# Second cross attention of a four-layer block: from seven slots a unit to four phases a unit

## The reference, cut to what matters

```python
q = layernorm(x, ln_q_g, ln_q_b) @ Wq * scale
k, v = jnp.split(media @ Wkv, 2, axis=-1)
sim = jnp.einsum('bhid,bhjd->bhij', q, k)
sim = jnp.where(media_mask[:, None, None, :], sim, neg_inf)
attn = jax.nn.softmax(sim, axis=-1)
out = jnp.einsum('bhij,bhjd->bhid', attn, v)
```

## Time and profile before

| what | value |
|---|---|
| time, median of 3 runs | 3631.37 us (3630.75 to 3647.57) |
| span of the profiled execution | 3628.6 us |
| the profiled execution's own time | not listed apart; its span is 2.8 us under the median |
| TensorE busy | 3390.8 us, 93% of the span |
| VectorE, ScalarE, GpSimd busy | 2019.1, 1846.1, 1589.9 us |
| second cross attention | from about 1633 to 3045 us of the span |

### The profile page before, as it was taken

The page is one execution under the profiler, slowest core; times in us unless marked ns, Lnnn a source line. Parts: engine busy times, 40 slices in busy tenths (PEclk is TensorE's granted clock), DMA queues, the critical chain, the costliest instruction groups (busy, mean ns, idle before and its releaser), DMA issues. The chain is left out here.

```text
span 3628.6 us, 74082 instructions
## 1 busy us (share of the span) xinstructions
PE 3390.8 (93%) x25048; PEld 2305.3 (64%) x25048; DVE 2019.1 (56%) x3324; ACT 1846.1 (51%) x3374; POOL 1589.9 (44%) x1421
## 2 busy tenths in 40 slices
PE   7798799898999799989999999999999998999997
PEld 5556544344444388866666666666666666878886
DVE  4465577776777454435555555555555553114454
ACT  2254277676776533335555555555555553333333
POOL 3213012221221011107777777777777775005554
PEclk9899799999999899999999999999999999999998
DMA  4784200000000222220000000000001003220200
GB/s 120 170 131 120 79 7 18 17 17 17 17 18 27 96 74 100 107 112 10 13 31 14 32 13 32 16 30 15 33 29 42 13 13 119 82 75 1 98 7 12
DMA packets 74751, 179.36 MB, mean 49 GB/s; under 512 B 14720, under 2 KB 44928, under 8 KB 68480
## 3 DMA queue, kind: packets, MB, share of 16 engines
q1 hardware_dynamic: 70240, 161.81, 14.7%
q0 software_dynamic: 4128, 12.60, 1.3%
HBM read 115.09 MB, written 59.26 MB: 48 GB/s over the span
## 5 line engine op out<-in xcount | busy, mean ns | idle before, releaser
L1654 POOL TENSOR_TENSOR cross_acc<-cross_acc,cross_probs 128x512 f32<-128x512 f32 (+1 forms) x704 | 921.4, 1309 | 159.9 <-ACT cross_probs L1717 118.6
L1717 ACT ACTIVATE cross_probs<-cross_s,cross_bias 128x512 f32<-128x512 f32 (+1 forms) x832 | 530.3, 685 | 488.9 <-PE cross_s L1936 487.1
L1813 DVE TENSOR_REDUCE cross_partmax<-cross_r 128x1 f32<-128x400 f32 (+1 forms) x1024 | 541.2, 570 | 334.3 <-PE cross_r L1906 316.0
L1256 DVE TENSOR_REDUCE cross_partmax<-cross_m 128x2 f32<-128x800 f32 (+1 forms) x512 | 497.0, 991 | 187.1 <-PE cross_m L1359 186.1
L1167 ACT ACTIVATE cross_probs<-cross_s 128x512 f32<-128x512 f32 (+1 forms) x832 | 453.9, 596 | 150.7 <-PE cross_s L1379 150.4
L1949 PE MATMUL cross_av<-cross_probs,cross_v 128*64 128x256 f32 (+1 forms) x3328 | 459.1, 394 | 0.0
L1949 PEld LDWEIGHTS cross_av<-cross_probs,cross_v 128*64 128x64 f32 (+1 forms) x3328 | 199.5, 136 | 173.2 <-ACT cross_probs L1717 77.3
L1106 POOL TENSOR_TENSOR cross_diag<-c_ident,cross_negmax 128x256 fp32r<-128x256 f32 x128 | 76.0, 615 | 497.6 <-DVE cross_negmax L1264 497.6
L1390 PE MATMUL cross_av<-cross_probs,cross_v 128*32 128x256 f32 (+1 forms) x3328 | 269.0, 395 | 10.2 <-ACT cross_probs L1167 9.0
L1802 DVE TENSOR_TENSOR cross_k_lo<-cross_r,cross_k_hi 128x400 fp32r<-128x400 f32 (+1 forms) x256 | 146.4, 572 | 192.4 <-ACT cross_k_hi L1695 192.4
L1930 PE MATMUL cross_s<-cross_q_hi,cross_k_hi 64*128 64x256 f32 (+1 forms) x1664 | 253.0, 299 | 0.0
(11 more groups left out here) (307 smaller groups left out, 6479.6 us busy)
## 6 DMA issues: line engine op xcount, KB each, us to landing
d_masked_ctx<-tail_ctx_split SPq DMA_DIRECT2D x8, 1602.0 KB, 5.3
d_self_qk<-selfproj_qk_split POOLq DMA_DIRECT2D x32, 256.0 KB, 5.5
self_qs<-d_self_qk SPq DMA_DIRECT2D x64, 128.0 KB, 8.0
self_ks<-d_self_qk SPq DMA_DIRECT2D x64, 128.0 KB, 8.5
d_cross<-tail_pr SPq DMA_DIRECT2D x8, 1024.0 KB, 4.6
cross_qp<-d_cross SPq DMA_DIRECT2D x64, 128.0 KB, 2.4
d_cross<-cross_out SPq DMA_DIRECT2D x64, 128.0 KB, 1.8
tail_attn<-d_cross SPq DMA_DIRECT2D x8, 1024.0 KB, 5.5
```

The source lines that it names most:

```text
L1256: nc.vector.tensor_reduce(partmax[:, :, jt // 2, jt % 2, i:i + 1], m_pair(sets[q], w), AX.X, ALU.max).then_inc(maxed, 1)
L1654: nc.gpsimd.tensor_tensor(acc[0:w, g % 2], left, probs[0:w, slot % NPB], ALU.add).then_inc(added, 1)
L1717: nc.scalar.activation(probs[0:w, (g * KT + t) % NPB], src_, ACT.Exp, scale=XHD ** -0.5, bias=bias[0:w, p, t:t + 1]).then_inc(probs_ready, 1)
L1813: nc.vector.tensor_reduce(partmax[:, m, i:i + 1], r_ps[MAX_BANK[q]][:, 0:KCH[i][1]], AX.X, ALU.max).then_inc(maxed, 1)
```

## The change

The unit is cut in four phases of two score sets each instead of seven slots, on all three engines. The sets are now ranges of two or one tiles, so that the groups 0 to 3, 4 to 6, 7 to 9 and 10 to 12 fill the phases, and a set's buffer is `s_ps[s % 2]`. On TensorE phase k runs: maxima 4k and 4k+1; scores of set 2k; maxima 4k+2 and 4k+3; scores of set 2k+1; value products of the group in front (in phase 0 those of the unit before, followed by its sums); in phase 3 the shift; key chunk k of `after`; one value tile. Keys now always use bank 1, value tiles bank 2, shift and sums bank 0. The start-up code keeps its banks, apart from the first scores, which move to phase 0. GpSimd and SyncE keep their order, and no instruction is added or dropped.

```diff
-        SETS = [range(t, min(t + 2, KT)) for t in range(0, KT, 2)]
+        SETS = [range(lo, hi) for lo, hi in ((0, 2), (2, 4), (4, 6), (6, 7), (7, 9), (9, 10), (10, 12), (12, 13))]
+        GROUPS = [range(0, 4), range(4, 7), range(7, 10), range(10, 13)]
-        K_BANK, V_BANK, SHIFT_BANK, SUM_BANK = (2, 1, 0, 2), (0, 2, 0, 1), 1, 1
-        MAX_BANK = (0, 1, 2, 0, 2, 0, 1, 2, 1, 2, 0, 1, 0, 1, 2, 0)
-        v_at, k_at = {1: (0,), 4: (1,), 6: (2, 3)}, {2: 0, 3: 1, 4: 2, 5: 3}
+        K_BANK, V_BANK, SHIFT_BANK, SUM_BANK = (1, 1, 1, 1), 2, 0, 0
+        MAX_BANK = (0, 1, 2, 0) * 4
```

ScalarE:

```diff
+                def phase(u, nxt, k, before):
                     after = nxt and following(nxt, NP)
+                    for s in (2 * k, 2 * k + 1):
+                        for t in SETS[s]:
+                            exponential(u, s, t)
+                    if after:
+                        k_high(after, k)
+                    made = value_tile(u, k)
+                    if made:
+                        v_tile(*made, r_ps[V_BANK])
+                    if before:
+                        copy_av(before)
+                        inverse_sum(before)
```

VectorE, in `step(u, nxt)`:

```diff
+                    for k in range(NQ):
+                        for q in range(4 * k, 4 * k + 4):
+                            maxima(nxt, q)
+                        if k == NQ - 1:
+                            diagonals(nxt)
+                            copy_shift(nxt)
+                        if after:
+                            k_low(after, k)
+                    if after:
                         queries(after)
```

TensorE:

```diff
+                def max_item(u, nxt, q, before):
+
+                    n, after, k = nxt[3], following(nxt, NP), q // 4
+                    if q == 0:
+                        pe.wait_ge(shifted, n + PRIME)
+                        pe.wait_ge(k_ready, (n + 1) * NC + PRIME)
+                    elif q == 2 and before and value_tile(before, NQ - 1):
+                        pe.wait_ge(v_ready, value_made(before, NQ - 1) + PRIME)
+                    elif q == 4:
+                        pe.wait_ge(ln_ready, n - 1 + PRIME)
+                        pe.wait_ge(maxed, n * NM + 4 + PRIME)
+                    elif q % 4 == 1 and k and after:
+                        pe.wait_ge(k_ready, (n + 1) * NC + k + PRIME)
+                    elif q % 4 == 2 and k and value_tile(u, k - 1):
+                        pe.wait_ge(v_ready, value_made(u, k - 1) + PRIME)
+                    elif q > 2:
+                        pe.wait_ge(maxed, n * NM + (q, q - 3, q - 3, q - 2)[q % 4] + PRIME)
+                    maxima(nxt, q)
+
+                def phase(u, nxt, k, before):
                     after = nxt and following(nxt, NP)
+                    if nxt:
+                        max_item(u, nxt, 4 * k, before)
+                        max_item(u, nxt, 4 * k + 1, before)
+                    scores(u, 2 * k)
+                    if nxt:
+                        max_item(u, nxt, 4 * k + 2, before)
+                        max_item(u, nxt, 4 * k + 3, before)
+                    scores(u, 2 * k + 1)
+                    if k:
+                        values(u, k - 1)
+                    elif before:
+                        values(before, NQ - 1)
+                        if nxt:
+                            pe.wait_ge(maxed, nxt[3] * NM + 4 + PRIME)
+                        sums(before)
+                    if nxt and k == NQ - 1:
                         shift(nxt)
+                    if after:
+                        pe.wait_ge(maxed, nxt[3] * NM + 4 * k + 2 + PRIME)
+                        k_chunk(after, k)
+                    made = value_tile(u, k)
+                    if made:
+                        pe.wait_ge(maxed, nxt[3] * NM + 4 * k + 3 + PRIME)
+                        v_tile(*made, r_ps[V_BANK])
```

More of the change, by code:

```diff
@@ L1581, in next_half, with value_tile @@
             return None if isinstance(b, int) and b == B - 1 else (b + 1, 1 - p, 0)
-        def value_tiles(u, s):
+        def value_tile(u, j):
             half_batch, share = next_half(u), v_share(u[2])
-            return [(half_batch, share[j], j) for j in v_at.get(s, ()) if j < len(share)] if half_batch else []
+            return (half_batch, share[j]) if half_batch and j < len(share) else None
         def value_count(u, j):
@@ L1736, in ahead @@
                     for i in range(NC):
-                        k_high(u, i)
+                        k_high(u, i, K_BANK_AHEAD)
                     for t in range(KT):
                         v_tile((0, 0, 0), t, ahead_bank(t))
[L1740 to L1746, removed]
-                    after = nxt and following(nxt, NP)
[L1748 to L1756, removed]
-                            exponential(nxt, t)
-                    if after and s in k_at:
-                        k_high(after, k_at[s])
-                    if s < NS - 1:
-                        for hb, t, j in made:
-                            v_tile(hb, t, r_ps[V_BANK[j]])
-                    if s == NS - 1:
-                        copy_av(u)
@@ L1773, in start, with step @@
+                def step(u, nxt):
+                    for k in range(1, NQ):
+                        phase(u, nxt, k, None)
+                    if nxt:
+                        phase(nxt, following(nxt, NP), 0, u)
+                    else:
+                        copy_av(u)
+                        inverse_sum(u)
                 def start(u):
                     ahead(u)
-                    slot(u, following(u, NP), 0)
+                    phase(u, following(u, NP), 0, None)
                 units(act, NP, start, step)
@@ L1835, in ahead @@
                     for i in range(NC):
-                        k_low(u, i)
+                        k_low(u, i, K_BANK_AHEAD)
                     for q in range(NM):
-                        maxima(u, q)
+                        maxima(u, q, MAX_BANK_AHEAD)
                     diagonals(u)
                     copy_shift(u)
-                    for i in range(3):
-                        k_low(second, i)
                     queries(second)
-                    k_low(second, 3)
+                    for i in range(NC):
+                        k_low(second, i, K_BANK_AHEAD)
                 def step(u, nxt):
@@ L1977, in ahead @@
                     pe.wait_ge(maxed, 15 + PRIME)
-                    k_chunk(second, 0)
+                    k_chunk(second, 0, K_BANK_AHEAD)
+                    k_chunk(second, 1, K_BANK_AHEAD)
                     pe.wait_ge(maxed, NM + PRIME)
@@ L2060, in step @@
                 def step(u, nxt):
-                    for s in range(1, NS):
-                        slot(u, nxt, s, None)
+                    for k in range(1, NQ):
+                        phase(u, nxt, k, None)
                     if nxt:
-                        slot(nxt, following(nxt, NP), 0, u)
+                        phase(nxt, following(nxt, NP), 0, u)
                     else:
+                        values(u, NQ - 1)
                         sums(u)
@@ L2069, in start @@
                     ahead(u)
-                    slot(u, following(u, NP), 0, None)
+                    phase(u, following(u, NP), 0, None)
                 units(pe, NP, start, step)
```

140 lines of the change are left out of this document (32 added, 108 removed).

## The result

The changed kernel takes 3890.79 us (median of 4 runs, 3888.2 to 3898.97); beside it the kernel before had 3634.71. The ratio is 1.0701, 95% interval 1.0677 to 1.0725: slower by 7.0%, 256 us.

What follows compares the result with a forecast made beforehand. TensorE's own sequence was taken to bound the kernel. Waits of 4.63 us a unit against 1.47 saved gave +185 us, clock falls +50; 235 on the span of 3628.6 gave 3863.6, median 3866, range 3780 to 3935.

Steps and rivals of the forecast that it cites:

- The work without waits: TensorE's four phases with three value tiles and no wait: 20.52 us a unit, a gain of 1.47.
- Phase 0 to 1, the logarithm: Maximum 4 waits for the logarithm, queued on ScalarE behind key, value-tile and products copies: 1.32 us a unit.
- Phases 1 to 2 and 2 to 3: Each phase's second maximum waits for bank 1, where the keys just lay: 0.56 us, twice a unit.
- The shift: In phase 3 TensorE's shift waits for VectorE's diagonal after the last reductions: 0.92 us a unit.
- Phase 3 to 0: Maximum 0 waits for key chunk 3, made just ahead, uncovered in three units of four: 1.27 us.
- GpSimd at no cost: GpSimd, 17.0 us a unit of 25, keeps its order and ends its last addition ahead of the sums: 0.
- The clock: TensorE's clock falls in about half of the units, 1.6 us each: 50 us, bounds 0, 105 and 210.
- Rival 1: The waits come as walked and the clock holds: 3816 us; chance 0.33.
- Rival 3: Waits smaller than walked, as copies and subtractions are ready earlier; with 1.5 of 4.63 us gone, 3723 us; chance 0.07.
- rival 4: Fewer switches between 64-row and full-row work decide, if new waits stay under 1.47 us a unit; all hidden, 3540; chance 0.05.

Runs made afterwards that it cites:

- y2_banks: Changed kernel, every phase with keys and value tile before products, shift last, high queries on ScalarE, maxima in banks 2, 1, 0, 2: 3590.41 us, ratio 0.9868.
- e2_log: Changed kernel with ScalarE taking the copy of the products and the logarithm ahead of the key copy in phase 0: 3828.34 us, ratio 1.0517.
- e4_keys: Changed kernel with key chunk and value tile ahead of the value products on TensorE in phases 1 and 2: 3802.17 us, ratio 1.0452.
- e6_scalar_q: Changed kernel with the high part of the queries made by ScalarE behind the last key copy, instead of by VectorE: 3857.46 us, ratio 1.0587.
- e3_fill: Changed kernel with extra TensorE matmuls, results never used, filling waits ahead of maximum 0, maximum 4 and the shift: 3841.32 us, ratio 1.0556.
- e5_keys3: Changed kernel with, in phase 3 alone, key chunk and any fourth value tile ahead of value products and shift on TensorE: 3901.46 us, ratio 1.0719.
- f1_three: Changed kernel with high queries before the shift's copy, logarithm before the key copy, keys before value products in phases 1 and 2: 3729.87 us, ratio 1.0251.
- e7_keys3_scalar_q: Changed kernel with phase 3's keys ahead of products and shift, and the high queries made by ScalarE: 3784.65 us, ratio 1.0389.

## Why the prediction came out as it did

Forecast 3866 in 3780 to 3935, slower; measured 3891. By its steps:

- **The work without waits, 20.52 us.** The unit of 25.55 less its waits (1.31 + 0.57 + 0.57 + 0.87 + 1.67 = 4.99) is 20.56. So this term held: a gain of 1.43 us, not 1.47. No run has this order free of waits; y2_banks, in another order, kept 0.87 of it.
- **Phase 0 to 1, the logarithm, 1.32.** Measured 1.31, and e2_log shows the queue on ScalarE as its cause.
- **Phases 1 to 2 and 2 to 3, 0.56 each.** Measured 0.57 (2.55 less 1.98 for phase 2); e4_keys took both away, with 1.13 for the two. Not all of it is seen as a late start of the scores: the exit behind them took 0.32 (2307.76 to 2308.08), and 0.21 in e4_keys.
- **The shift, 0.92.** Measured 0.87. The chain that gives it has a slip of 0.04 (two reductions of 0.54 from 2.19 end at 3.27, not 3.31), and it prices the diagonal at the 1.35 of the trace before, which already held a wait for GpSimd; without it the wait would be some 0.1. So the size was right and its reason was half known.
- **Phase 3 to 0, 1.27.** Measured 1.67. This is the step that failed: "`queries` stays at the unit's end with a unit's slack". Maximum 0 needs the high queries as well as the low keys, and the copy stands behind them on VectorE. The chain of waits names it (L1790), and e6_scalar_q, which takes it away, leaves a wait of 1.37: 0.30 is the copy's. The other 0.10 is mostly the way from the low keys back to TensorE, taken as 0.05 and 0.13 in e6_scalar_q. Together 0.40 a unit, 25 us in 62 units, as much as the forecast was short; what the other terms were off by, 0.05 at most, cancels. What I could not have read from the rows before is that the copy's end hangs on GpSimd.
- **GpSimd at no cost.** Wrong for the same reason: its last addition of the unit ends at 7.30 in phase 3, ahead of the sums as stated, but not ahead of the copy; and its additions lengthen the diagonal. The prediction counted GpSimd as a queue of its own; that its instructions lengthen VectorE's was not in the account.
- **The clock, a fall in half the units, 1.6 us each, 50 us.** 34 falls in 62 units, 1.5 us each between the two heaps; e3_fill measures 53 us. The length of a fall and the place of the idle time were worked out, but "half of the units" was a choice between bounds of 0 and 105 us, and that it came so near is luck: e5_keys3, with a unit just as long, had 49 falls. Rival 1, the walked waits with the clock held, came out 75 us short: 25 for the longer units and 50 for the clock.
- **Rival 3, smaller waits, and rival 4, faster.** The waits were real, and f1_three shows that they add. Rival 4's mechanism is real too, as y2_banks shows, but its condition (under 1.47 us of waits) was missed by 3.5 us.

## What to carry to other kernels

When an engine is busy without a gap, an order with fewer switches pays only if no result is asked for right after its input was issued: follow each chain across the engines from the last matmul to the bank's release, and put the consumer at least that long behind. Read every wait of the instruction at the head of a phase, not only the one that the bank needs; the copy of the queries was the second wait of the same matmul. A duration read from a trace may hold a wait of its own, as the diagonal's 1.35 us did; compare it with the same instruction where its neighbours are idle. And where waits of about a microsecond lie side by side, count the clock as well, since filling them with useless matmuls alone gave 53 us back.

## What the runs showed of the hardware

VectorE's copy of a float32 tile from SBUF to SBUF (128x256) takes 0.28 us when GpSimd's additions are short, and 1.37 us in the middle of full ones, ending as a rule 0.15 us after an addition does. Its float32 product of two SBUF operands (the diagonal, 128x512) takes 0.69 us and 1.35 to 1.44 us, ending 0.54 to 0.55 us after an addition. The Trainium skill, "SBUF — State Buffer", section "SBUF: two separate sides", has the rule that VectorE, in a mode that uses two ports or with two SBUF inputs, and GpSimd lock the shared pair of ports against each other: the instruction that starts first holds it for its whole length, and the other is shut out. The traces agree, with those numbers. In the kernel before the same copy had a median of 0.41 us and TensorE waited for none of them.

TensorE's clock fell with TensorE busy 1.82 of 3.40 us and no single wait above 1.83 us; in e5_keys3 it fell 49 times, with a single wait of 2.11 to 2.25 us a unit at that place. With the first of the two neighbouring waits nearly gone and the second at 1.2, and some 3.8 us of waits a unit left (e7_keys3_scalar_q), it fell in no unit. What exactly brings it down was not measured.
